# A pre-norm transformer block on eight cores: the residual input loaded in two halves one step ahead, and the FFN's first product issued two blocks ahead

## The reference

```python
def attn(x):                         # x (4, 4096, 1024), 16 heads of 64
    q, k, v = split(x @ W_attn)
    att = polymax(where(causal, q @ k.T / 8, -inf))   # polynomial in place of a softmax
    return concat_heads(att @ v) @ W_proj

def ffn(x):                          # low rank: 1024 -> 256 -> 4096 -> 256 -> 1024
    H = gelu((x @ U1) @ V1 + b1)
    return (H @ U2) @ V2 + b2

x = x + attn(layernorm(x))
x = x + ffn(layernorm(x))
```

## Time and profile before

| what | value |
|---|---|
| time before, median of 3 runs | 2149.38 us (2148.69 to 2149.43) |
| the profiled execution, its own time | 2146.54 us |
| its span on the slowest core (core 3) | 2145.0 us |
| spans of the eight cores | 2130.6 to 2145.0 us |
| TensorE busy, share of core 3's span | 1304.2 us, 61% |
| VectorE busy | 1257.3 us, 59% |
| ScalarE busy | 760.9 us, 35% |
| projection stage on core 3, first matmul to end of the last | 1658.91 to 1747.95 us |
| FFN on core 3 | about 1893 to 2145 us |

### The profile page before, as it was taken

One profiled execution on the slowest core, in us unless ns is written; L12 is line 12 of the kernel. 1 busy time (PEld: TensorE's weight loads), 2 busy tenths in 40 slices (PEclk: granted clock), 3 DMA queues, 4 the chain that ended last, 5 costly groups with the idle time before them and its releaser, 6 DMA issues.

```text
span 2145.0 us, 22487 instructions; the slowest of 8 cores (2130.6 to 2145.0 us)
## 1 busy us (share of the span) xinstructions
PE 1304.2 (61%) x6880; PEld 472.6 (22%) x6880; DVE 1257.3 (59%) x2171; ACT 760.9 (35%) x1074; POOL 0.2 (0%) x4
## 2 busy tenths in 40 slices
PE   3423277478676767677655557667771641477776
PEld 0001133243222221111112223222220210023332
DVE  3558433245889999999972223689993223344422
ACT  1100000002677877777750000477771000143333
POOL 0000000000000000000000000000000000000000
PEclk8755698798556667777877789656665875588888
DMA  5445211200000000000001100000003333001111
GB/s 161 157 128 186 79 40 40 79 1 1 1 1 1 1 1 1 1 1 1 1 26 54 54 25 1 1 1 1 1 1 106 110 111 104 0 0 40 40 40 40
DMA packets 37333, 87.67 MB, mean 41 GB/s; under 512 B 1889, under 2 KB 7266, under 8 KB 37218
## 3 DMA queue, kind: packets, MB, share of 16 engines
q1 hardware_dynamic: 30498, 75.75, 11.0%
q10 hardware_dynamic: 6720, 10.49, 1.6%
HBM read 77.85 MB, written 8.39 MB: 40 GB/s over the span
## 4 chain that ended last, share of the span: by engine, by line
PE 39%; DVE 28%; issue 16%; DMA 12%; ACT 4%; DVEq 1%; SPq 0%; ACTq 0%
DVE poolD L721 15%; DMA poolD<-W_attn 6%; PE ps L753 5%; PE ps L688 3%; PE ps L1051 3%; PE ps L864 3%; PE ps L612 3%; PE ps L634 3%; PE ps L1032 3%; PE ps L592 3%; PE ps L849 3%; PE ps L948 2%; DMA poolC<-x_own_t 2%; ACT poolD L708 2%; DVE poolD L733 2%
## 5 line engine op out<-in xcount | busy, mean ns | idle before, releaser
L708 ACT ACTIVATE poolD<-ps 128x1024 bf16<-128x1024 f32 (+3 forms) x640 | 560.9, 900 | 851.6 <-PE ps L688 676.3
L721 DVE SCALAR_TENSOR_TENSOR poolD<-poolD 128x1024 bf16<-128x1024 bf16 (+3 forms) x640 | 648.8, 1062 | 45.0 <-ACT poolD L708 23.2
L753 PE MATMUL ps<-poolD,poolA 128*64 128x512 bf16 (+3 forms) x1280 | 311.6, 472 | 227.6 <-DVE poolD L721 116.7
L688 PE MATMUL ps<-poolB,poolA 64*128 64x512 bf16 (+3 forms) x1280 | 287.0, 475 | 33.8 <-ACT poolD L713 16.4
L753 PEld LDWEIGHTS ps<-poolD,poolA 128*64 128x64 bf16 x1280 | 94.1, 119 | 420.5 <-issue 420.5
L1043 ACT ACTIVATE poolC<-ps,sb_b1s 128x512 bf16<-128x512 f32 x128 | 87.9, 687 | 124.3 <-PE ps L1032 124.0
L713 ACT ACTIVATE poolD<-ps,consts 128x256 bf16<-128x256 f32 x256 | 124.1, 485 | 0.0
L688 PEld LDWEIGHTS ps<-poolB,poolA 64*128 64x128 bf16 x1280 | 65.1, 102 | 239.0 <-issue 237.9
L948 PE MATMUL ps<-poolC,poolD 128*128 128x512 bf16 x256 | 65.8, 425 | 62.4 <-DVE poolD L898 39.2
L364 ACT ACTIVATE poolD<-ps 1x512 f32<-1x512 f32 x4 | 2.3, 587 | 245.9 <-PE ps L360 245.9
L761 PE MATMUL ps<-poolD,poolA 128*64 128x128 bf16 x512 | 86.6, 306 | 0.0
(11 more groups left out here) (100 smaller groups left out, 1155.5 us busy)
## 6 DMA issues: line engine op xcount, KB each, us to landing
poolD<-x_t SPq DMA_DIRECT2D x8, 2048.0 KB, 10.0
poolA<-x_t SPq DMA_DIRECT2D x8, 2048.0 KB, 9.7
poolD<-W_attn SPq DMA_DIRECT2D x12, 1024.0 KB, 5.0
poolD<-W_attn SPq DMA_DIRECT2D x16, 512.0 KB, 3.7
poolC<-x_own_t SPq DMA_DIRECT2D x4, 2048.0 KB, 8.2
y<-poolC SPq DMA_DIRECT2D x4, 2048.0 KB, 7.4
poolD<-W_proj SPq DMA_DIRECT2D x8, 512.0 KB, 3.8
poolD<-U ACTq DMA_DIRECT2D x5, 512.0 KB, 4.5
```

Source lines behind the costliest of these rows:

```text
L688: e.matmul(o, l, r, skip_group_check=True, start=True, stop=True, tile_position=tp),
L708: e.activation(o, i, AF.Relu), inc="S")
L721: e.scalar_tensor_tensor(o, i, 0.01, i, ALU.add, ALU.mult),
L753: e.matmul(o, l, r, skip_group_check=True, start=st, stop=True, tile_position=tp),
```

## The change

It touches two places. In the projection stage the load of 2 MB per block becomes two loads of 1 MB, one for feature blocks 0 to 3 and one for 4 to 7, in the same single buffer `xown`. Both halves of the first block are issued ahead of the loop. The first half of block `c + 1` is issued after the fourth addition of block `c`, the second half after its eighth. VectorE waits for a half just before the first addition that reads it. In the FFN, `emit_h` runs two blocks ahead of the gelu instead of one: h(1) is issued before the four f32 matmuls, and in the loop h(fc + 2) stands where h(fc + 1) stood, between the gelu's issue and the `U2` matmuls of `fc`. TensorE's list becomes h(0), h(1), the f32 matmuls, h(2), u(0), h(3), u(1) and so on. The number of PSUM banks (two) and of slots in `hb2` (two) stays.

```diff
+        x_own_src = x_own_t.rearrange("(dc p) t -> p dc t", p=128)
+        xdd = {}
+
+        def xo_dma(c, h):
+            xdd[(c, h)] = b.dma(xown[:, 4 * h:4 * h + 4, :],
+                                x_own_src[:, 4 * h:4 * h + 4, c * 512:(c + 1) * 512])
+        xo_dma(0, 0)
+        xo_dma(0, 1)
         for c in range(4):
-            dd = b.dma(xown[:, :, :],
-                       x_own_t.rearrange("(dc p) t -> p dc t", p=128)[:, :, c * 512:(c + 1) * 512])
-            b.wait("vector", dd, 16)
             for dcol in range(DC):
                 bk = dcol % 2
+                if dcol % 4 == 0:
+                    b.wait("vector", xdd[(c, dcol // 4)], 16)
                 b.wait("tensor", "V", evac2[bk])
...
-            b.wait("sync", "V", b.cnt["V"])
+                if dcol in (3, 7) and c + 1 < 4:
+                    b.wait("sync", "V", b.cnt["V"])
+                    xo_dma(c + 1, dcol // 4)
...
             hfence[0] = emit_h(0)
+            hfence[1] = emit_h(1)
             if c + 1 < 4:
                 emit_ln2_normalize(c + 1)
             for fc in range(32):
...
-                if fc + 1 < 32:
-                    hfence[fc + 1] = emit_h(fc + 1)
+                if fc + 2 < 32:
+                    hfence[fc + 2] = emit_h(fc + 2)
                 b.wait("tensor", "S", gelu_S[fc % 2])
```

## The result

| what | before | after |
|---|---|---|
| median of the runs beside each other | 2150.45 us (10 runs) | 2123.47 us (9 runs) |
| ratio | | 0.988, 95% interval 0.9857 to 0.9902 |
| the profiled execution, its own time | 2146.54 us | 2123.97 us |
| spans of the eight cores | 2130.6 to 2145.0 us | 2107.2 to 2122.4 us |

The kernel is 1.2% faster, by 27.0 us on the medians. The forecast was 2121.0 us and 28.4 us. In the profiled execution the slowest core is now core 5; before it was core 3.

The account below looks back on a forecast made before the run. Loads of `x_own_t` and TensorE's slow restart were taken to bound the projection stage, latency the FFN loop. Gains of 27.9 us (projection) and 0.5 us (FFN) off 2149.4 us gave 2121.0 us, range 2114 to 2126.

Parts of the forecast that it names:

- The halves are in time: Projection, blocks 1 to 3: each 1 MB half takes about 5.0 us, its buffer is free for 7.9, nothing is exposed.
- Blocks 1 to 3 as one dense stretch of 41.5 us at 0.216 us per matmul: Projection: with loads hidden, TensorE runs 192 matmuls without a break, as in the key projection.
- The rival of a lower clock in the denser stretch: Projection: dense matmuls on all eight cores are not granted their clock; 2162 us with blocks 1 to 3 low; 2 in 100.
- The current limiter at 13/16: Projection: milder clock rival, 13/16 of 2.4 GHz, near 2133 us; a rate between levels, 2126 to 2140 us, 3 in 100.
- Block 0: Projection's first block: no gain on core 0; core 3 gains 26.9 us in the stage at worst, 32.3 at best.
- The sum: Whole kernel: 27.9 us from the projection plus 0.5 from the FFN, 28.4 us off 2149.4, giving 2121.0 us.
- The range: Whole kernel: 2114 to 2126 us, taking in the late halves, leaving out the FFN gain and the clock.
- The FFN: FFN loop: only the order within the pair is swapped; gelu waits for its output slot, two steps stay 1.96 us.
- The term for the head of the blocks: FFN, head of blocks 0 to 2: h(1) ahead of the f32 matmuls saves 0.3 us per block, 0.5 taken in all.
- The FFN edit works as it looks: FFN rival: gelu bound by h alone, step 0.864 us instead of 0.98, 14 us more, 2107 us; 5 in 100.
- The halves come late: Projection rival: each half costs 8.2 us and is partly exposed at six places, 4 us, 2125 us; 9 in 100.

Follow-up runs that it names:

- p1: Kernel with both edits, but both halves of the next block are issued together after the eighth addition; 2142.12 us, ratio 0.9957 to the kernel before.
- p3: Kernel with both edits, plus one more 1 MB load into unused memory ahead of each of the six halves of blocks 1 to 3; 2125.89 us.
- p4: Kernel with both edits, plus two more 1 MB loads into unused memory ahead of each of the six halves of blocks 1 to 3; 2144.93 us.
- e3: Kernel with both edits, but hb2 has four slots instead of two; 2104.85 us, ratio 0.9785 to the kernel before.
- e4: Projection edit and four slots for hb2, but the FFN's old order, h one step ahead; 2119.61 us, ratio 0.9867 to the kernel before.
- f2: Kernel with both edits and two slots, but h(1) moved back behind the four f32 matmuls; 2122.45 us, ratio 0.9868 to the kernel before.

## Why the prediction was right, step by step

**The halves are in time.** Right, with the price: 5.3 us was measured (the median on core 5) where 5.0 had been taken from a load of the same size, against 7.9 us of room. No wait for `x_own_t` was left in blocks 1 to 3, and `p1`, `p3` and `p4` show it is this lead that counts.

**Blocks 1 to 3 as one dense stretch of 41.5 us at 0.216 us per matmul.** Right. The stage took 56.7 to 58.3 us from the start of its first matmul to the end of its last, on the eight cores, against the 56.7 of the key projection that was the model. By core the gains in this stage were 26.2, 27.4 and 28.1 us on cores 0, 2 and 5, where the prediction has 26.4, 26.5 and 26.8.

**The granted clock.** The rival of a lower clock in the denser stretch fell: 1.00 was granted from the fourth us to the last on core 5, and on all eight cores over 41 us of the stage. The current limiter at 13/16 that the Trainium skill describes ("TensorE: Matmul & The Clock Gate", Part 1) did not show, with all eight cores in matmuls that stand back to back for over 50 us; the trace does not agree with the page here.

**Block 0.** On core 3 the prediction left open whether the first half would be in time. It was, on every core, and core 3 gained 31.5 us in the stage, near the upper bound of 32.3. The first half landed 6.0 to 8.8 us after its issue and the second 8.3 to 11.8, so the order of issue holds here too. The reading of the earlier trace rows against it, that the load behind delayed `W_proj`'s last piece (5.09 us), is not borne out: in the same profile that piece took 3.5 to 3.8 us on cores 1, 2, 4 and 6, with the same load behind it.

**The sum.** On the medians it was 2.5 us short, 2121.0 against 2123.47. Of this 1.1 us is the kernel before, which took 2150.45 us beside the changed one and not 2149.4. The other 1.4 us is the gain, 27.0 instead of 28.4, and the stages say where: the projection gave 27.6 (27.9 had been taken), the FFN cost 1.1 instead of giving 0.5. By core the sum was much further off, and that the slowest came out so near is in part luck. Core 0, forecast as the slowest with core 3, has a span of 2107.2 us where the sum had 2116.8; core 5 has 2122.4 where it had 2115.0. Core 5 started the stage 3.5 us later than in the profile before, its stage was 1.3 us shorter than forecast, and what comes behind, which the prediction held to be as long as before, took 5.2 us more on this core. The prediction took every core's start from one profile, where it moves by up to ten us between executions, and left out core 7, whose 2142.2 us before were more than core 5's; it is the second slowest after, at 2119.3. The range held all of this.

**The FFN.** The main point was right: the pair is swapped, the output slot takes over the wait, and two steps stay at 1.95 us. `e3` and `e4` show the slot and the order as the two halves of one condition. The term for the head of the blocks was wrong in sign: -0.5 us was taken, +1.0 us measured in the loops (142.2 against 141.2). The 0.3 us per block is there where the clock does the same in both kernels: in block 0 the loop takes 34.57 us on seven cores after and 34.86 on six before. But in blocks 1 and 2 TensorE's clock stays low for longer, and `f2` shows that the place of h(1) does it. The prediction had counted matmuls there at one rate.

**The rivals.** "The FFN edit works as it looks" would have been 14 us more and needed a third thing, the slots; `e3` gives about what it priced (15.6 us in the loops). "The halves come late" is what `p3` builds, at 2.4 us where 4 had been priced.

The version that beats both kernels is `e3_four_slots`: 2104.85 us, 45 us under the kernel before.

## What to carry to other kernels

A producer is as far ahead as the smallest ring in its cycle lets it be. Before issuing an operation earlier, list every buffer that the cycle passes (here the PSUM bank and the output slot), and ask for each who frees it and where that stands in the in-order list; if the last of them is still freed by the same instruction, nothing but the order changes. A single buffer can be loaded ahead in parts without a second copy, as each part is free from its last reader in one round to its first reader in the next; that time against the landing time of a part decides, and it can be read off the trace before. A stop of TensorE can cost more than its length: behind the stops of 3.4 us and more seen here the restart cost another 1.4 to 3.2 us, with one exception, behind those of 0.9 to 1.7 us at most 1.1.

## What the runs showed of the hardware that was not expected

After a stop of 3.5 us the next 48 matmuls took 13.4 us instead of 10.4 (`p1_halves_late`, core 7), so a stop half as long as the one before the change (6.6 us) had a restart as dear. Over all cores, behind 24 stops of 3.4 to 4.2 us in that kernel 48 matmuls took 11.8 to 13.6 us, once 10.5; behind the stops of blocks 1 to 3 before the change, 6.2 to 6.9 us, they took 11.8 to 13.4. Behind the stops in `p3_double_load`, 0.9 to 1.7 us, they took 10.5 to 11.5.

Four f32 matmuls whose stationary operand has one row took the granted clock from 1.00 to 0.50, with TensorE busy throughout; the block without them kept 1.00. How long it stayed there changed with the place of h(1): on core 2, block 1, some 3.5 us with h(1) behind them and about 7 us with h(1) ahead. In block 0 the loop was shorter with h(1) ahead, so the length does not follow from the number of matmuls ahead alone.
